# Weight units reordered and loaded at other places, and the context of the next tile moved to the tile's beginning, in a fused attention and ternary FFN kernel

## Chip, cores and metric

One Trainium2 chip, all 8 NeuronCores, one launch. Each core computes half of the rows of one batch element, with no traffic between cores. The metric is the device time of the slowest core in microseconds. The kernel before takes 1146.7 us, the median of 3 timed runs (1144.61 to 1150.81).

## The reference, cut to what matters

```python
x = hidden_states                     # (4, 4096, 1024), D = 1024, 16 heads of 64
h = layernorm(x)
q = softmax((h @ Wq.T + bq) @ Wfq.T + bfq)      # over all 1024 features
k = softmax((h @ Wk.T + bk) @ Wfk.T + bfk)
v = h @ Wv.T + bv
ctx = (q k^T / rowsum) v              # no softmax over positions: linear attention
x = x + ctx
a = act_quant(layernorm(x))           # 127 / max|row|, rounded
W' = weight_quant(W)                  # scale by 1/mean|W|, round, clip to -1, 0, 1
g = silu(a @ w_gate'.T); u = a @ w_up'.T        # INNER = 4096
x = x + act_quant(g * u) @ w_down'.T
```

Each weight matrix of the FFN can be quantised only when the mean of |W| over the whole matrix is known, so it has to be read through once for the mean and a second time for the quantised values.

## The kernel before

**Work and tiles.** A core holds 2048 rows of its own (16 tiles of 128, `TQ`) and also reads the other 2048 rows of its batch element, since keys and values need all 32 tiles (`TKV`). The first phase walks over 32 slots i. Slot i projects the values V(i) (from slot 8 on, `NE`), one of the items CQ(0) to CQ(8) that fold the two query matrices into one (slots 5 to 13, `cq_slot`), or the query logits Q(t) (slots 16 to 26), then the key logits K(i+1), and adds k^T v of tile i into PSUM (`pe_kv`, named KV below). An item is 16 matmuls of 128x512. VectorE adds the bias and takes the maximum, ScalarE takes the exponential (`ac_ek`, EK) and scales the values (`ac_ve`, VE). The second phase runs the FFN over the 16 own tiles: per tile 8 pairs G, U of 8 matmuls each (oc 0 to 7), and, from tile 3 on (`LAG` = 3), the down projection of the tile three back, 64 matmuls.

**Weight units.** The FFN weights come in 48 units of 1 MB each (16 per matrix; w = 0 gate, 1 up, 2 down). A unit (1, w, u) is pass 1: load it and let ScalarE sum |W| (`unit_ac`, an Abs of 1.9 us). A unit (2, w, u) is pass 2: load it again, let GpSimd scale it (`unit_gp`), and let ScalarE write the sign as fp8. Units 13 to 15 of gate and up are kept (`NRET` = 3, tile `keep`) between the passes, in the space that `wg8` and `wu8` take later, which is also the space of the attention weights and of `stage`. A kept unit's load therefore waits (`ready`, L378) for CQ(8) in the case of gate, and for the last two casts of the attention weights in the case of up. All other units rotate through 4 buffers `wst` (3 in the FFN phase), and the load of one waits until the one before it in its buffer has been used.

**Order.** `units` (L330 to L336) is one list. A planner (L346 to L352) puts its first 74 units into slots of the first phase by estimated slot length; the first 6 (`NPRE`) are handled ahead of the slots. With that rule the slots before hold 2 units in slots 5 to 7, 3 in slots 8 to 12, 3 in slot 13 (number 28, then the kept gate units 29 and 30), and about 3 in each of 16 to 26 and 2 in 27 to 29. The 22 remaining units go into FFN tiles 0 to 3 at the steps listed in `ffn_units` (L452). The matrix means are finished in a chain ScalarE, VectorE, TensorE, VectorE (`mean_dv1`, `mean_pe`, `mean_dv2`); `mean_at` (L459) puts it one slot after the matrix's last unit: slot 9 for up, slot 15 for gate. The mean of down stands in tile 1, at oc 1 on VectorE and after oc 2 on TensorE.

**Queues.** Every engine has one instruction list that it runs in order. SyncE issues nearly all loads (L751 to L763): in slot i first the activation tile i + 4, then the units of the slot. An issue whose semaphore isn't there yet holds all that stand behind it in SyncE's list. In the FFN ScalarE issues the loads of the down units itself, behind the unit three before.

**Steps touched in the FFN.** `pe_ctx(t+1)` computes the attention output of the next tile in 3 parts into PSUM banks `KB[0..2]`; `dv_ctx` normalises them and adds them to the residual (`cm`, `x2`). Before, they stand after oc 0 of tile t, and from tile 4 on (`t > LAG`) two parts share a bank, `KB[0]`, so part 2 waits for part 0's `cm`. `ac_hq` converts the previous tile's hidden values behind GpSimd's scaling (`gp_hr`) and, in tiles 1 to 3, stands ahead of the first two `ac_silu`.

## Time and profile before

| | value |
|---|---|
| timed runs, slowest core | 1146.7 us median (1144.61 to 1150.81, n = 3) |
| the profiled execution | 1136.11 us, span of its slowest core 1134.4 us |
| spans of the 8 cores in it | 1122.7 to 1134.4 us |
| TensorE matmul busy | 1071.1 us, 94% of the span |
| VectorE, ScalarE, GpSimd busy | 627.7, 500.3, 204.0 us |
| moved by DMA | 193.36 MB, mean 170 GB/s |

The profile is one execution on its slowest core, core 3. The 90 unit loads of 1 MB, the 20 MB of attention weights and most of the activations pass in the first 570 us. The profiled execution lies 10.6 us below the median of the timed ones.

### The profile page before, as it was taken

What the parts mean: (1) busy time and instruction counts of PE and PEld (TensorE: products, weight loads), DVE (VectorE), ACT (ScalarE), POOL (GpSimd) and SP (SyncE); (2) the same over time, 40 slices, a digit from 0 to 9 for tenths busy, and PEclk for the clock granted to TensorE, in tenths of its full rate; (3) what the DMA queues carried; (4) which work ended last, traced back from release to release, by engine and by line L of the source; (5) the groups of instructions that cost most, each with busy time, mean ns of one, the idle gap of its engine ahead of it and who ended that gap; (6) DMA issues with size and microseconds to landing.
All of it is one profiled execution on the core that took longest, in us unless ns stands there. A gap on an engine that the chain in (4) does not pass through costs nothing.

```text
span 1134.4 us, 13495 instructions; the slowest of 8 cores (1122.7 to 1134.4 us)
## 1 busy us (share of the span) xinstructions
PE 1071.1 (94%) x5414; PEld 501.3 (44%) x5414; DVE 627.7 (55%) x1133; ACT 500.3 (44%) x603; POOL 204.0 (18%) x132
## 2 busy tenths in 40 slices
PE   4898889979999999897989999999999999999998
PEld 2343444434444544343434444444444444444443
DVE  4525655566767667775745744644744644744311
ACT  3545867568888837465442222222222222222110
POOL 0000001022443320454322021021021021011010
PEclk9998999999999999899999999999999999999999
DMA  8996999669979966779961451451341341241240
GB/s 274 313 318 197 344 307 336 239 237 306 343 240 331 317 173 195 190 198 240 173 128 38 84 121 38 85 121 38 84 121 38 84 121 38 75 93 40 55 110 38
DMA packets 202318, 193.36 MB, mean 170 GB/s; under 512 B 169872, under 2 KB 173968, under 8 KB 194832
## 3 DMA queue, kind: packets, MB, share of 16 engines
q1 hardware_dynamic: 180448, 168.39, 53.3%
q10 hardware_dynamic: 21808, 24.12, 7.0%
q8 instruction: 42, 0.69, 0.3%
q14 instruction: 20, 0.16, 0.1%
HBM read 142.16 MB, written 29.36 MB: 151 GB/s over the span
## 4 chain that ended last, share of the span: by engine, by line
PE 65%; DVE 11%; ACT 10%; DMA 10%; issue 3%; POOL 1%; SPq 1%; ACTq 0%; DVEq 0%; POOLq 0%
PE ps L664 33%; PE ps L644 19%; PE ps L481 9%; DMA wst<-wuT 4%; ACT ek L1227 2%; DMA wst<-wdT 2%; ACT wst L411 2%; DVE nm L864 1%; DVE bnst L829 1%; ACT wu L425 1%; DVE lg L860 1%; DMA keep<-wuT 1%; ACT wg L425 1%; DVE hmid L1172 1%; ACT eq L1253 1%
## 5 line engine op out<-in xcount | busy, mean ns | idle before, releaser
L664 PE MATMUL ps<-wg,aqT 128*128 128x512 fp8e4 x1024 | 244.5, 382 | 4.1 <-DVE aqT L1139 2.6
L664 PE MATMUL ps<-wu,aqT 128*128 128x512 fp8e4 x1024 | 244.0, 381 | 2.3 <-DVE hmid L1172 2.2
L1296 ACT ACTIVATE silu<-ps,l 128x512 f32<-128x512 f32 x128 | 87.7, 686 | 325.8 <-PE ps L664 315.1
L1172 DVE SCALAR_TENSOR_TENSOR hmid<-ps,l,silu 128x512 f32<-128x512 f32 x128 | 95.8, 748 | 141.7 <-PE ps L664 109.0
L664 PEld LDWEIGHTS ps<-wu,aqT 128*128 128x128 bf16 x1024 | 100.5, 98 | 126.3 <-DVE hmid L1172 4.3
L664 PEld LDWEIGHTS ps<-wg,aqT 128*128 128x128 bf16 x1024 | 98.5, 98 | 117.3 <-DVE aqT L1139 3.8
L1346 POOL TENSOR_SCALAR hmid<-hmid,hsc 128x1024 f32<-128x1024 f32 x64 | 70.4, 1118 | 316.9 <-DVE hsc L1193 316.9
L481 PE MATMUL ps<-wck,xT 128*128 128x512 bf16 x512 | 121.5, 393 | 0.8 <-ACT vst L1244 0.8
L397 POOL TENSOR_SCALAR wst<-wst,msum 128x2048 f32<-128x2048 f32 x42 | 84.3, 2012 | 210.4 <-DMA wst<-wuT 112.6
L1164 DVE SCALAR_TENSOR_TENSOR xr<-ps,hsc,xr 128x512 f32<-128x512 f32 x32 | 24.0, 751 | 168.1 <-PE ps L644 168.1
L481 PE MATMUL ps<-wv,xT 128*128 128x512 bf16 x448 | 101.1, 379 | 0.0
L1306 ACT ACTIVATE hqs<-hmid 128x1024 bf16<-128x1024 f32 x64 | 66.9, 1056 | 70.3 <-POOL hmid L1346 69.0
L644 PE MATMUL ps<-wd,hqTa 128*128 128x512 fp8e4 x384 | 85.9, 384 | 3.7 <-ACT wd L425 3.7
L411 ACT ACTIVATE wst<-wst 128x2048 f32<-128x2048 f32 x42 | 79.9, 1903 | 12.9 <-DMA wst<-wuT 8.2
L481 PEld LDWEIGHTS ps<-wck,xT 128*128 128x128 bf16 x512 | 51.1, 102 | 66.2 <-issue 7.7
L1180 DVE TENSOR_REDUCE hmx<-hmid 128x1 f32<-128x1024 f32 x64 | 78.1, 1220 | 2.2
L1339 POOL TENSOR_TENSOR xr<-xr,bvb 128x1024 f32<-128x1024 f32 x16 | 37.6, 2354 | 183.4 <-DMA xr<-x_own 183.4
L644 PE MATMUL ps<-wd,hqTb 128*128 128x512 fp8e4 x320 | 69.9, 379 | 0.0
L481 PE MATMUL ps<-wfT,wnat 128*128 128x512 bf16 x256 | 60.1, 395 | 5.3 <-ACT wfT L311 2.2
L481 PEld LDWEIGHTS ps<-wv,xT 128*128 128x128 bf16 x448 | 42.7, 98 | 46.5
L644 PEld LDWEIGHTS ps<-wd,hqTa 128*128 128x128 bf16 x384 | 37.8, 99 | 50.8 <-ACT wd L425 4.7
L860 DVE TENSOR_TENSOR lg<-ps,bkc 128x1024 f32<-128x1024 f32 x32 | 39.0, 1218 | 36.8 <-PE ps L481 32.1
(107 smaller groups left out, 1112.9 us busy)
## 6 DMA issues: line engine op xcount, KB each, us to landing
wst<-wuT SPq DMA_DIRECT2D x26, 1024.0 KB, 12.5
wst<-wgT SPq DMA_DIRECT2D x26, 1024.0 KB, 11.2
wst<-wdT ACTq DMA_DIRECT2D x19, 1024.0 KB, 5.8
xr<-x_own SPq DMA_DIRECT2D x32, 512.0 KB, 6.9
s_hq<-hqs SPq DMA_DIRECT2D x32, 512.0 KB, 4.1
wst<-wdT SPq DMA_DIRECT2D x13, 1024.0 KB, 7.8
xr<-x_oth SPq DMA_DIRECT2D x16, 512.0 KB, 13.7
y<-xr SPq DMA_DIRECT2D x16, 512.0 KB, 3.4
```

The source lines that it names most:

```text
L397: gp(lambda e: e.tensor_scalar(b, b, msum[:, 4 + w:5 + w], ROUND32, op0=ALU.mult, op1=ALU.add), [at("unit", unit_id[1, w, u]) if wslot_of[ ...
L411: ac(lambda e: e.activation(o, b, ACTF.Abs, bias=0.0, scale=1.0, accum_out=absc[:, k:k + 1], saturate=False), [at("wld", n), last_junk[0] ...
L481: pe(lambda e, h=h, c=c, l_=l_, r_=r_: e.matmul(AB[b][:, 512 * h:512 * h + 512], l_, r_, start=(c == 0), stop=(c == CH - 1)), (list(after) ...
L644: pe(lambda e, c=c, b=b, o=o: e.matmul(KB[1 + h], b[:, o:o + 128], wd8[:, c * D + 512 * h:c * D + 512 * h + 512], start=(c == 0), stop=(c ...
L664: pe(lambda e, c=c: e.matmul(out, a[:, c * 128:c * 128 + 128], w8[:, c * DI + 512 * oc:c * DI + 512 * oc + 512], start=(c == 0), stop=(c = ...
L860: dv(lambda e: e.tensor_tensor(o, b, bias[...], op=ALU.add), after, done)
L1172: dv(lambda e: e.scalar_tensor_tensor(hmid[:, 512 * oc:512 * oc + 512], U[oc % 2], l2[:, s + 6:s + 7], sl, op0=ALU.mult, op1=ALU.mult), [a ...
L1180: dv(lambda e: e.tensor_reduce(hmx[:, s2 + k:s2 + k + 1], hmid[:, D * k:D * k + D], axis=AX, op=ALU.max, apply_absolute_value=True), [at(" ...
L1296: ac(lambda e: e.activation(silu[:, (oc % 2) * 512:(oc % 2) * 512 + 512], G[oc % 2], ACTF.Silu, bias=0.0, scale=l2[:, s + 5:s + 6]), [at(" ...
L1306: ac(lambda e: e.activation(hqs[:, g * D:(g + 1) * D], hmid[:, g * D:(g + 1) * D], ACTF.Copy, bias=-ROUND32, scale=1.0), [at("hr", t, g)] ...
L1339: gp(lambda e: e.tensor_tensor(xf(t), xf(t), bvb[...], op=ALU.add), [at("x2in", t), at("biases")], ("xb", t))
L1346: gp(lambda e: e.tensor_scalar(o, o, hsc[:, k:k + 1], ROUND32, op0=ALU.mult, op1=ALU.add), [at("hs", t)], ("hr", t, g))
```

## The change

Six edits, all in the order of work; no instruction of the arithmetic is added or dropped.

1. `NPRE` falls from 6 to 3: three units, not six, are read ahead of EK(0) on ScalarE, and three more move into the slots. Four casts of attention weights move ahead of the first key steps on VectorE.
2. The list `units` is reordered: the second-pass use of the kept up units now stands ahead of the first-pass reading of the kept gate units.
3. The loads of the kept units are issued in slot 3 (up) and slot 13 (gate), behind the slot's activation tile and ahead of the slot's other units.
4. The means of up and gate are taken two slots after the last unit, not one. By the planner's rule the slots become: slot 4: number 3; slots 5 to 7: two each; slot 8: 10, 11, 12; slot 9: the kept up units 13 to 15; slots 10 to 12: 16 to 24; slot 13: 25, 26, 27, 28; slot 14: 29, 30 (kept up, pass 2); slot 15: 31 and 32; slot 16: 33 to 35; slot 21: four units (48 to 51) where there were three; slot 29: three (71 to 73) where there were two. Mean of up in slot 11, of gate in slot 18.
5. In FFN tiles 1 to 3 the context of the next tile stands at the beginning of the tile, on TensorE and VectorE, in three separate banks, now for tile 4 also.
6. The mean of down is asked for at the start of tile 1 on VectorE and after oc 1 on TensorE. Tile 1 takes 5 down units where it took 4, tile 3 takes 5 where it took 6. In tiles 1 to 3 ScalarE puts the silu between the two `ac_hq` of the step.

```diff
@@ -33,7 +33,7 @@
 NWF = 3
 NP1 = 10
 NRET = 3
-NPRE = 6
+NPRE = 3
 LAG = 3
 NXF = 6
 
@@ -327,9 +327,11 @@
 
 
 
-    units = [(1, w, u) for w in (1, 0) for u in range(16)]
     kept = list(range(16 - NRET, 16))
-    own = [(2, w, u) for w in (1, 0) for u in kept + list(range(16 - NRET))]
+    rest = list(range(16 - NRET))
+    units = [(1, 1, u) for u in rest + kept] + [(1, 0, u) for u in rest]
+    units += [(2, 1, u) for u in kept] + [(1, 0, u) for u in kept]
+    own = [(2, 1, u) for u in rest] + [(2, 0, u) for u in kept + rest]
     for u in range(NP1):
         own[4 * u + 3:4 * u + 3] = [(1, 2, u)]
     units += own
@@ -451,12 +453,12 @@
 
     ffn_units = {}
     n1 = NA
-    for t, at_oc in enumerate([(1, 2, 3, 4, 5, 6), (3, 4, 6, 7),
-                               (2, 3, 4, 5, 6, 7), (2, 3, 4, 5, 6, 7)]):
+    for t, at_oc in enumerate([(1, 2, 3, 4, 5, 6), (2, 3, 4, 6, 7),
+                               (2, 3, 4, 5, 6, 7), (2, 3, 4, 5, 6)]):
         ffn_units[t] = {oc: n1 + k for k, oc in enumerate(at_oc)}
         n1 += len(at_oc)
     assert n1 == len(units)
-    mean_at = {unit_slot[unit_id[1, w, 15]] + 1: w for w in range(2)}
+    mean_at = {unit_slot[unit_id[1, w, 15]] + 2: w for w in range(2)}
 
     def xsrc(i):
         t, src = (i, x_oth) if i < TQ else (i - TQ, x_own)
@@ -646,7 +648,7 @@
                 wd8[:, c * D + 512 * h:c * D + 512 * h + 512],
                 start=(c == 0), stop=(c == 31)),
                [at("hqT", t, c // 16), at("unit", unit_id[2, 2, c // 2]),
-                at("y", t - 1, h) if t else at("cm", LAG, 1 + h)],
+                at("y", t - 1, h) if t else at("cm", LAG + 1, 1 + h)],
                ("down", t, h) if c == 31 else None)
 
     for p in range(3):
@@ -670,27 +672,30 @@
     WL = max(unit_id[2, w, u] for w in range(2) for u in range(16))
 
     def ctx_bank(t, part):
-        return KB[part] if t <= LAG else (KB[0], T, KB[0])[part]
+        return KB[part] if t <= LAG + 1 else (KB[0], T, KB[0])[part]
 
     for t in range(TQ):
+        if 0 < t <= LAG:
+            for k in range(3):
+                pe_ctx(t + 1, k, KB[k], at("cm", t, 2) if k == 0 else None)
         for oc in range(8):
             b = oc % 2
             pe_half(t, oc, G[b], wg8,
                     gfree[b] + [at("aqT", t), at("unit", WL)], ("G", t, oc))
             pe_half(t, oc, U[b], wu8, ufree[b], ("U", t, oc))
             gfree[b], ufree[b] = [at("silu", t, oc)], [at("h", t, oc)]
-            if t == 1 and oc == 2:
+            if t == 1 and oc == 1:
                 mean_pe(2, t_free[0])
                 t_free[0] = at("mean", 2)
-            if t + 1 < TQ and oc == 0:
-                pe_ctx(t + 1, 0, ctx_bank(t + 1, 0), at("cm", t, 2))
-                if t + 1 <= LAG:
+            if oc == 0 and (t == 0 or LAG < t < TQ - 1):
+                pe_ctx(t + 1, 0, KB[0], at("cm", t, 2))
+                if t == 0:
                     pe_ctx(t + 1, 1, KB[1], None)
                     pe_ctx(t + 1, 2, KB[2], None)
                 else:
                     pe_ctx(t + 1, 1, T, t_free[0])
                     t_free[0] = at("cm", t + 1, 1)
-            if LAG < t + 1 < TQ and oc == 1:
+            if LAG < t < TQ - 1 and oc == 1:
                 pe_ctx(t + 1, 2, KB[0], at("cm", t + 1, 0))
             if t + 1 < TQ and oc == 6:
                 pe_at(t + 1)
@@ -734,8 +739,7 @@
         unit_load(n)
     for n in range(NV, NV + 8):
         load_chunk(n)
-    for n in range(4, NPRE):
-        unit_load(n)
+    unit_load(4)
 
     def load_xf(t):
         if t < 4:
@@ -759,8 +763,13 @@
             load_x(i + 4)
         elif i >= TKV - 4:
             load_xf(i + 4 - TKV)
+        for w in (1, 0):
+            if i == (13, 3)[w]:
+                for u in kept:
+                    unit_load(unit_id[1, w, u])
         for n in slot_units[i]:
-            unit_load(n)
+            if n > 4 and wslot_of[n] is not None:
+                unit_load(n)
 
     def load_eld(t):
         free = (at("ctx", t - 2, 2) if t >= 2 else
@@ -995,23 +1004,26 @@
     cke(4)
     cke(5)
     unit_ac(1)
-    unit_ac(2)
     cke(6)
     cke(7)
-    for n in range(3, NPRE):
-        unit_ac(n)
+    unit_ac(2)
     dv(lambda e: e.tensor_tensor(bkc[...], bkc[...], AB[item_bank["BK"]],
                                  op=ALU.add),
        [at("BK"), at("bfk")], ("BKe",))
+    cast_chunk(NV)
+    cast_chunk(NV + 1)
     dv_tk(0)
+    cast_chunk(NV + 2)
     dv_tk(1)
+    cast_chunk(NV + 4)
     for i in range(TKV):
         dv_rz(i)
         if NE <= i + 2 < TKV:
             dv_xh(i + 2)
         if i < 4:
             for n in range(NV + 4 * i, NV + 4 * i + 4):
-                cast_chunk(n, "v")
+                if n not in (NV, NV + 1, NV + 2, NV + 4):
+                    cast_chunk(n, "v")
         if NE <= i + 3 < TKV:
             dv_stats(i + 3)
         if i in mean_at:
@@ -1194,16 +1206,20 @@
            [at("hc", t)], ("hs", t))
 
     for t in range(TQ):
+        if t == 1:
+            mean_dv1(2)
+        if 0 < t <= LAG:
+            for k in range(3):
+                dv_ctx(t + 1, k, ctx_bank(t + 1, k))
         for oc in range(8):
             dv_h(t, oc)
             if t == 1 and oc == 1:
-                mean_dv1(2)
                 mean_dv2(2)
             if t + 1 < TQ:
-                if oc == 0:
+                if oc == 0 and not 0 < t <= LAG:
                     dv_ctx(t + 1, 0, ctx_bank(t + 1, 0))
                     dv_ctx(t + 1, 1, ctx_bank(t + 1, 1))
-                if oc == 1:
+                if oc == 1 and not 0 < t <= LAG:
                     dv_ctx(t + 1, 2, ctx_bank(t + 1, 2))
                 if oc == 2:
                     dv_ln2a(t + 1)
@@ -1267,7 +1283,8 @@
         ac_ve(i)
         if i < 4:
             for n in range(NV + 4 * i, NV + 4 * i + 4):
-                cast_chunk(n, "a")
+                if n not in (NV, NV + 1, NV + 2, NV + 4):
+                    cast_chunk(n, "a")
         for n in us[0:1]:
             unit_ac(n)
         if NE <= i + 3 < TKV:
@@ -1316,12 +1333,8 @@
         for oc in range(8):
             if early and oc < 2:
                 ac_hq(t - 1, 2 * oc)
-                if oc == 0:
-                    ac_hq(t - 1, 1)
-                    ac_silu(t, 0)
-                else:
-                    ac_silu(t, 1)
-                    ac_hq(t - 1, 3)
+                ac_silu(t, oc)
+                ac_hq(t - 1, 2 * oc + 1)
             else:
                 ac_silu(t, oc)
             if t + 1 < TQ and oc == 5:
```

## Rows read from the trace of the kernel before

**Rows 1.** Cores: span and mean granted clock of some cores.

```profile
core 0: 1123.3 us, clock 0.991
core 3: 1134.4 us, clock 0.983
```

**Rows 2.** Who waited for whom, TensorE: line, releaser, us in total, times, longest us.

```profile
PE ps L435 <- DVE msum L430: 9.7, 3, 3.7
```

**Rows 3.** Short windows: busy us per engine (x instructions), granted clock, DMA share, GB/s.

```profile
96.00:100.00 4.00, 0.27 (x2) 0.00 (x0) 3.30 (x5) 1.46 (x3) 0.00 (x0) 0.80 0.00 0
212.00:216.00 4.00, 4.00 (x21) 1.81 (x19) 2.17 (x5) 3.49 (x6) 0.00 (x0) 1.00 0.02 4
220.00:224.00 4.00, 4.00 (x21) 1.78 (x19) 2.21 (x3) 1.32 (x1) 0.00 (x0) 1.00 0.96 360
```

**Rows 4.** Timeline of TensorE, slots 0 to 10: start, us, what, [idle before <- releaser].

```profile
101.64 1.05 PE L548 MATMUL ps<-vst,ek 128*128 128x129 bf16 x8 [5.37 <-ACT vst L1244]
...
167.02 0.59 PE L435 MATMUL ps<-msum,ones 128*128 128x1 f32 x2 [3.66 <-DVE msum L430]
...
174.78 3.62 PE L481 MATMUL ps<-wv,xT 128*128 128x512 bf16 x16
```

**Rows 5.** Timeline of ScalarE: a late unit before EK(0), the last kept up unit.

```profile
93.50 1.91 ACT L411 ACTIVATE wst<-wst 128x2048 f32<-128x2048 f32 x1 [1.12 <-DMA wst<-wuT]
...
161.45 1.91 ACT L411 ACTIVATE junk<-keep 128x2048 fp8e4<-128x2048 f32 x1 [1.37 <-DMA keep<-wuT]
```

**Rows 6.** SyncE's queue: what it waited for, and its issues around slot 13.

```profile
SPq L251 <- PE ps L481: 18.0, 1, 18.0
...
197.38 0.33 SPq L251 DMA_DIRECT2D wst<-wgT  x1
215.71 1.97 SPq L251 DMA_DIRECT2D keep<-wgT  x2
```

**Rows 7.** Timeline of ScalarE, slot 13: number 28, the second kept unit, EK(14).

```profile
213.43 1.90 ACT L411 ACTIVATE wst<-wst 128x2048 f32<-128x2048 f32 x1
...
225.24 1.91 ACT L411 ACTIVATE junk<-keep 128x2048 fp8e4<-128x2048 f32 x1 [0.56 <-DMA keep<-wgT]
...
227.15 1.13 ACT L1227 ACTIVATE ek<-lg,nm 128x1024 bf16<-128x1024 f32 x1
```

**Rows 8.** Timeline of TensorE: KV(14), the mean of gate, V(16).

```profile
229.90 0.64 PE L548 MATMUL ps<-vst,ek 128*128 128x129 bf16 x8 [2.95 <-ACT vst L1244]
...
237.58 0.38 PE L435 MATMUL ps<-msum,ones 128*128 128x1 f32 x2 [3.14 <-DVE msum L430]
237.82 5.30 PE L481 MATMUL ps<-wck,xT 128*128 128x512 bf16 x16
...
243.88 3.62 PE L481 MATMUL ps<-wv,xT 128*128 128x512 bf16 x16
```

**Rows 9.** Timeline of ScalarE in a query slot: two signs behind EQ.

```profile
336.01 3.89 ACT L425 ACTIVATE wg<-wst,cst 128x2048 fp8e4<-128x2048 f32 x2 [0.46 <-ACT eq L1253]
```

**Rows 10.** The chain that ended last: start, us, what, around the loads that TensorE waited for.

```profile
216.08 9.08 DMA keep<-wgT
...
378.80 11.72 DMA wst<-wgT
...
551.05 17.55 DMA wst<-wdT
```

**Rows 11.** Timeline of TensorE, FFN tiles 1 to 3 and the first down projection.

```profile
470.88 0.59 PE L435 MATMUL ps<-msum,ones 128*128 128x1 f32 x2 [2.91 <-DVE msum L430]
...
537.74 0.29 PE L623 MATMUL ps<-kvs,eld 128*128 128x130 bf16 x2 [4.44 <-DVE tmp L1061]
...
572.74 9.20 PE L644 MATMUL ps<-wd,hqTa 128*128 128x512 fp8e4 x34 [2.07 <-ACT wd L425]
```

**Rows 12.** Timeline of VectorE, tile 1: two equal residual adds of the context.

```profile
465.87 1.68 DVE L1067 TENSOR_TENSOR xr<-xr,tmp 128x384 f32<-128x384 f32 x1
...
468.28 0.56 DVE L1067 TENSOR_TENSOR xr<-xr,tmp 128x384 f32<-128x384 f32 x1
```

## Prediction

> **What bounds the kernel now.** I read in this order: cores, the engine table, TensorE's waits, then the timelines of TensorE, ScalarE and SyncE slot by slot, and last short windows for the DMA share. The slowest core needs 1134.4 us, the fastest about 11 us less, with clocks within 0.01 [rows 1]: the cores differ by their waits. TensorE is busy 94% of the span, so a gain can only come out of its stalls and out of the slow stretch that follows a stall. Those lie in two places. In slots 0 to 15 they end on late weight units or on a mean (9.7 us in three mean waits, the third of them in the FFN) [rows 2, 4, 8]. In FFN tiles 1 to 3 and the first down projection they end on the mean of down, on context part 2 (4.44 us) and on down weights [rows 11]. From tile 4 on TensorE doesn't stall and no edit reaches it. After a stall an item that takes 3.6 us otherwise took 5.30 [rows 8]: the granted clock there stood at the lower of its two levels, 1.2 GHz, as it does in a window after the first stall (0.80 on average, falling to half) [rows 3]. So a stall of 3 us costs about 5.
>
> The reader should see a third thing, since the change moves it: SyncE's queue. It waited once for 18.0 us for TensorE [rows 6]. That is the load of the kept gate units, held until CQ(8) ends at 215.5 us. In the windows before its end the DMA share is 0.02 [rows 3], and yet nothing stalled until then, because the loads up to number 28 had been issued at 197.4, ahead of the wait [rows 6], and ScalarE could begin number 28 at 213.4 [rows 7].
>
> **The change, part by part.** The sum stands against the profiled execution, 1136.1 us; the same difference is then put on the median of 1146.7, which lies 10.6 higher, as I find no term that would differ there.
>
> *Front, slots 0 to 10.* Before, EK(0) waits behind number 5, which ends at 95.4 [rows 5], and KV(0) begins at 101.64 after 5.37 us of idle [rows 4]. With three units ahead, EK(0) needs only the first maximum, some 3 us earlier, and so does KV(0). Four casts move forward, so three 0.5 MB chunks are fetched while the DMA queues stood empty (share 0.00 from 96 to 100) [rows 3]. But this is not yet time won, because slots 4 to 9 run at the pace of the loads. The volume up to the last up unit is the same as before. At 360 GB/s [rows 3] a unit takes 2.9 us and with the small transfers between them about 3.2. I counted the queue's idle time in the new order. It still idles until about 102, since chunk 35 needs a cast in slot 0. It idles again for nearly 4 us at about 110 to 114, because the kept up loads wait in slot 3 for the last cast with all later activation tiles and units behind them. That is 12 us of idle against 10.5. The last up unit (now number 12) lands at about 161 to 163, where before the last kept unit was begun at 161.45 [rows 5]. What is really won is the mean: TensorE idled 3.66 us for it at 167.0 [rows 4], and in slot 11 it will be there. But K(10) reuses the bank of V(9) and cannot start before about 166 for that reason, so only 1 us is left. I take −1.0 for the start of V(10) (174.78 before) [rows 4]. Bounds: +3, if the two idle stretches of the queue add up fully, and −6, the 3.66 with its slow item.
>
> *Slot 13.* This is the largest term, and it goes against the change. SyncE's list now reads: tile 17, three kept gate loads (wait for CQ(8)), then 25, 26, 27 and 28. Before, 25 to 28 stood ahead of that wait. ScalarE's list reads VE(13), 25, 26, 27, 28, EK(14), and behind EK(14) stand VE(14) and KV(14), at which TensorE stops. So all 7 MB must land after CQ(8) ends, call it T. First data flows about 2 us after the issue (kept load issued at 215.7, share 0.96 by 220) [rows 3, 6], then 7 x 2.9 = 20.3, then 2.1 for the last Abs: EK(14) starts at T + 24.4. KV(14) follows 2.75 later (227.15 to 229.90) [rows 7, 8], at T + 27.2. Before it was 229.90 - 215.5 = T + 14.4. The term is +12.8. Two kept loads took 9.08 us from issue to landing with small transfers between [rows 10], which agrees with 2.9 each. TensorE has items for 11 us after T and then stalls for some 16. Bounds: +9 (a rate of 420 GB/s and an early start) and +16 (3.4 us per unit).
>
> Here a rule of the Trainium skill speaks against the change. The row shows the queue silent for 18.0 us in front of one held load [rows 3, 6]. "DMA: Bandwidth & Descriptors", section "Anatomy of one DMA", says that a semaphore wait happens on the issuing sequencer before dispatch and that the DMA engines do not wait; the trace agrees. Were the wait held in the DMA queues instead, 25 to 28 would pass it and the whole change would gain about 13 us.
>
> *Slots 14 to 16.* The mean of gate moves from slot 15 to 18. Before, from KV(14) to V(16) it took 243.88 - 229.90 = 14.0 us, with 3.14 of idle and a slow item of 5.30 [rows 8]. Now V(15), slow after the stall (about 5.5), K(16) 3.5 and two short groups give 10.8. The term is −3.2, bounds −4 and −1.
>
> *Slots 21 and 29.* In the query slots the loop over ScalarE sets the pace: EQ, then the units, then EK. Two signs take 3.89 us behind EQ [rows 9]. A fourth unit in slot 21 adds one sign, +1.9 (bound 0 if EQ still waits). In slot 29 a third unit comes in ahead of EK(30); its load is issued after a unit of slot 28 and needs some 11.7 us [rows 10], so it just arrives, and its Abs adds +2.0 (bounds 0 and +3).
>
> *FFN tiles 1 to 3.* Ideal is 3.46 us per pair. Tile 1 (454 to 492) loses 2.91 of idle for the mean of down and 2.9 of slow matmuls behind it [rows 11]. The mean's first step now runs before VectorE's context work. What is late next: the first hidden product, which waits for the context. Its three parts take 6.1 us, since a residual add takes up to 1.68 while GpSimd runs, where an equal one takes 0.56 [rows 12]; TensorE then waits about 1.6 us for the buffer U. Net −5.0. Tile 2 starts from a VectorE that is less behind: it takes 33.1 us where 28.6 is ideal, and of these 4.5 us in small waits I take off 3. In tile 3 the 4.44 us for context part 2 [rows 11] and the slow pairs after it (1.8) go, since three banks are used; against it VectorE's context again stands ahead of the first product, 2.6. What is then late are the down units. The last one before was issued at 551.05 and took 17.55 us to land [rows 10], among the transposes of the hidden values; TensorE waited 2.07 for the last of them [rows 11]. With all tiles earlier, and one unit more fetched in tile 1, the last one lands some 12 us earlier by my count (about 557), and the first down projection ends near 569 instead of 581.8. The term is −12.5. Bounds: −17 (only 10 of the 27 us lost here remain) and −4 (the down loads do not come earlier; only tile 1's wait, less its new one, is kept).
>
> Sum: −1.0 + 12.8 − 3.2 + 1.9 + 2.0 − 12.5 = 0.0. So 1136.1 stays, and on the median 1146.7; I say 1147.
>
> **Rivals.** *A, slower: down weights take the place of the waits removed.* The 22 down units and the transposes share the queues, and loads issued among transposes took 17.55 us against 9.08 without [rows 10]. If TensorE reaches tile 3 earlier but the last down unit lands at most 4 us earlier than now, TensorE waits for it in the first down projection. It decides from the moment at which the last sign comes later than the 31st matmul of that projection. Then the FFN gives −5 and the sum is +7.5: 1154. For it: waits there on ScalarE's signs already [rows 11]. Against it: the DMA share in tiles 0 and 1 leaves room to fetch earlier.
>
> *B, faster: the front gives more.* If the earlier chunks and the kept up units, loaded before the rest, keep the queues full, then VE(9) comes 4 to 5 us earlier, and the stall in slot 13 is shorter by a faster burst (9 instead of 12.8). The sum is −8: 1139. For it: 10 us of empty queue before 102 [rows 3]. Against it: the wait for the last cast in SyncE's list.
>
> *C, the stall of slot 13 doesn't come.* It would need CQ(8) to end long before ScalarE reaches number 25. Before, CQ(8) ended 2.1 us after ScalarE began slot 13's first unit [rows 6, 7]. The sum would be −13: 1134. I give it little.
>
> **How the numbers follow.** Forecast (terms near their values, within 5 us of zero): 0.46. A with its neighbours (also a longer burst in slot 13): 0.27. B: 0.22. C: 0.05. The likeliest case has its own range of 1141 to 1152. For 8 in 10 the range must take in A's 1154 and B's 1139 with the bounds of slot 13 and of the FFN: 1137 to 1158. Differences under 0.5% (5.7 us) can't be told from none here. Faster by more: 0.27. Within: 0.46. Slower by more: 0.27.
>
> **What the changed kernel's profile would show.** Slot 13: ScalarE idle ahead of four Abs with the releaser DMA wst<-wgT, and TensorE idle for about 16 us before a KV with a slow item behind it. Mean waits of up and gate: gone. V(10) within 3 us of 174. KV(14) near 242, V(16) near 252 to 254. Tile 1: no wait for msum, a wait of 1 to 2 us for hmid. Tile 3: no wait for tmp. The first down projection ends about 0 to 2 us from 581.8 in absolute time. The prediction would be wrong first if the burst of slot 13 cost under 9 or over 16 us, next if the first down projection still waited over 5 us for a sign.

## The result, and the profile after

The changed kernel is slower. Its median is 1165.88 us (1161.16 to 1229.43, 4 runs), against 1145.65 us (1143.39 to 1150.81, 4 runs) for the kernel before on the same chip; the ratio is 1.0156, 95% interval 1.0104 to 1.0209. The prediction was 1147 us with a range of 1137 to 1158, so the time lies outside it. Some executions were disturbed, with a lower granted clock on part of the cores: the ratios here leave out those far above the rest, and of the profiled execution of b2_casts_only (below), whose cores 0, 1, 4 and 5 ran at about 0.81 up to 280 us, only the other four cores are read. The profiled execution took 1161.16 us. The head of its page, then two of its cores with span and mean granted clock:

```profile
span 1159.6 us, 13495 instructions; the slowest of 8 cores (1132.8 to 1159.6 us)
```

```profile
core 3: 1144.2 us, clock 0.982
core 4: 1159.6 us, clock 0.971
```

The slowest core is now core 4. The cores lie up to 27 us apart, where before it was 12. To see where the time comes from I read the same instants off TensorE's timeline of every core and took means over the eight cores of a profiled execution. KV(i) is the start of the 8 short matmuls of that name; "tile 4" is the start of FFN tile 4's matmuls, behind the first down projection. Means in us, and the difference on core 3 alone, the core from whose trace the prediction was made:

| stretch | before | after | difference | on core 3 | predicted |
|---|---|---|---|---|---|
| span start to KV(9) | 170.6 | 173.2 | +2.6 | −0.9 | −1.0 (at V(10)) |
| KV(9) to KV(13) | 45.1 | 45.2 | +0.1 | +0.1 | 0 |
| KV(13) to KV(14) | 10.7 | 26.2 | +15.5 | +16.7 | +12.8 |
| KV(14) to KV(18) | 46.3 | 44.8 | −1.5 | −1.1 | −3.2 |
| KV(18) to KV(22) | 46.6 | 49.1 | +2.5 | +3.8 | +1.9 |
| KV(22) to start of the FFN | 105.0 | 105.3 | +0.3 | +0.7 | +2.0 |
| FFN to tile 4 | 151.2 | 147.2 | −4.0 | −9.6 | −12.5 |
| all up to tile 4 | 575.6 | 591.2 | +15.6 | +9.7 | 0.0 |

Such means differ between two profiles of the same code. Up to the FFN b4_before_short_down (below) is the kernel before, instruction for instruction, and its KV(9) stands at 173.1, its start of the FFN at 428.5, where the kernel before has 170.6 and 424.3. A difference of 2 or 3 us between two single profiles is therefore not certain.

Behind tile 4 nothing differs: core 3 before needs 552.6 us from there (1134.4 − 581.8), core 4 after the same (1159.6 − 607.0). Three places carry the result.

*Slot 13.* Core 3 of the changed kernel: SyncE's issues, ScalarE, TensorE (start, us, what, [idle before <- releaser]), then windows as in [rows 3].

```profile
214.93 2.49 SPq L251 DMA_DIRECT2D keep<-wgT  x3
217.46 2.53 SPq L251 DMA_DIRECT2D wst<-wgT  x4
...
233.00 1.91 ACT L413 ACTIVATE wst<-wst 128x2048 f32<-128x2048 f32 x1 [20.22 <-DMA wst<-wgT]
...
241.15 1.91 ACT L413 ACTIVATE wst<-wst 128x2048 f32<-128x2048 f32 x1 [0.45 <-DMA wst<-wgT]
...
245.81 1.05 PE L550 MATMUL ps<-vst,ek 128*128 128x129 bf16 x8 [19.64 <-ACT vst L1260]
...
247.50 5.58 PE L483 MATMUL ps<-wv,xT 128*128 128x512 bf16 x16
```

```profile
212.00:216.00 4.00, 4.00 (x20) 1.79 (x19) 2.18 (x4) 0.78 (x2) 0.00 (x0) 1.00 0.02 4
216.00:220.00 4.00, 4.00 (x32) 2.32 (x31) 1.80 (x3) 0.00 (x0) 0.00 (x0) 1.00 0.73 221
220.00:224.00 4.00, 4.00 (x20) 1.83 (x19) 1.46 (x2) 0.00 (x0) 0.00 (x0) 1.00 0.99 311
224.00:228.00 4.00, 2.17 (x11) 0.78 (x8) 0.00 (x0) 0.00 (x0) 0.00 (x0) 1.00 0.96 260
228.00:232.00 4.00, 0.00 (x0) 0.00 (x0) 0.00 (x0) 0.00 (x0) 0.00 (x0) 0.87 1.03 307
232.00:236.00 4.00, 0.00 (x0) 0.00 (x0) 0.00 (x0) 2.64 (x5) 0.00 (x0) 0.50 0.99 332
236.00:240.00 4.00, 0.00 (x0) 0.00 (x0) 0.00 (x0) 3.05 (x3) 0.00 (x0) 0.50 0.95 380
```

The queue is empty until CQ(8) ends (share 0.02), and then seven loads are issued within 5 us. ScalarE, which before was at its first unit of the slot at 213 [rows 7], waits 20.22 us, and TensorE stands for 19.64. While it stood the granted clock fell to 0.50, the lower of its two levels (1.2 GHz), and the first item after the stall took 5.58 us instead of 3.6, as one did after a smaller stall before [rows 8].

*Slot 5.* Of this stall the prediction says nothing. Core 3, SyncE, VectorE, TensorE:

```profile
113.14 1.27 SPq L251 DMA_DIRECT2D keep<-wuT  x3
114.46 2.29 SPq L251 DMA_DIRECT2D xr<-x_oth  x2
...
129.04 1.29 DVE L838 BATCH_NORM_STATS2 bnst<-xr 128x6 f32<-128x512 f32 x2 [9.15 <-DMA xr<-x_oth]
...
131.72 5.44 PE L483 MATMUL ps<-wfT,wnat 128*128 128x512 bf16 x16 [11.05 <-DVE wcq L910]
```

Three kept up units are issued ahead of activation tiles. VectorE waits for a tile, and TensorE for a result that VectorE forms behind that wait. On the mean KV(4) comes 4.4 us earlier than before, and KV(5) 6.0 us later.

*FFN.* Who waited for whom, TensorE, from the start of the FFN to tile 4 (us in total, times, longest). First the kernel before, core 3:

```profile
PE ps L623 <- DVE tmp L1061: 4.4, 1, 4.4
PE ps L644 <- ACT wd L425: 3.7, 2, 2.1
PE ps L435 <- DVE msum L430: 2.9, 1, 2.9
```

Then the changed kernel, core 4:

```profile
PE ps L666 <- ACT silu L1313: 18.7, 3, 10.9
PE ps L646 <- ACT wd L427: 3.1, 1, 3.1
```

Core 3 of the changed kernel has the same kind of wait:

```profile
PE ps L666 <- ACT silu L1313: 11.8, 4, 6.0
```

The waits that the edits aimed at are gone: no `tmp` (context part 2), no `msum` (mean of down). Another takes their place, which the kernel before has on a small scale (1.4 us in total on core 3, 3.3 on core 4). It reads best as a chain, core 4 in tile 3:

```profile
555.62 1.97 POOL L399 TENSOR_SCALAR wst<-wst,msum 128x2048 f32<-128x2048 f32 x1 [17.11 <-DMA wst<-wdT]
...
557.63 2.00 ACT L427 ACTIVATE wd<-wst,cst 128x2048 fp8e4<-128x2048 f32 x1 [14.66 <-POOL wst L399]
...
560.13 0.69 ACT L1313 ACTIVATE silu<-ps,l 128x512 f32<-128x512 f32 x1 [0.51 <-ACT wd L427]
...
560.88 3.59 PE L666 MATMUL ps<-wg,aqT 128*128 128x512 fp8e4 x8 [10.89 <-ACT silu L1313]
```

A down unit's load lands late, GpSimd waits for it, the sign on ScalarE waits for GpSimd, and the silu that TensorE needs stands behind the sign in ScalarE's list.

The last of the 22 down units shows how the stream of loads as a whole moved. GpSimd's scaling of it on core 3, in the kernel before and in the changed one:

```profile
568.68 1.97 POOL L397 TENSOR_SCALAR wst<-wst,msum 128x2048 f32<-128x2048 f32 x1 [0.71 <-DMA wst<-wdT]
```

```profile
575.84 1.97 POOL L399 TENSOR_SCALAR wst<-wst,msum 128x2048 f32<-128x2048 f32 x1 [3.78 <-DMA wst<-wdT]
```

Counted from the core's own start of the FFN (426.9 and 446.2) these are 141.8 and 129.6 us, 12.2 less. On the mean of the cores they are 138.1 and 133.4, only 4.7 less, and tile 4 follows 13 to 14 us later (151.2 and 147.2), as the 64 matmuls of the first down projection alone take 13.98 us. So the end of this stretch moves with the stream of down loads, be it through a wait in the projection or through the silus ahead of it.

### The profile page after: what moved, and what is told of

It reads as the page before. It is cut to its first block, busy times and chain, and to the rows that moved or that the text cites. A ratio compares the mean times of both kernels' runs of the same rounds, so it can differ in the third digit from the quotient of the medians.

```text
span 1159.6 us, 13495 instructions; the slowest of 8 cores (1132.8 to 1159.6 us)
## 1 busy us (share of the span) xinstructions
PE 1069.4 (92%) x5414; PEld 502.3 (43%) x5414; DVE 616.4 (53%) x1133; ACT 499.4 (43%) x603; POOL 206.4 (18%) x132
## 4 chain that ended last, share of the span: by engine, by line
PE 64%; DMA 13%; ACT 10%; DVE 9%; issue 2%; POOL 1%; SPq 1%; ACTq 0%; DVEq 0%; POOLq 0%
PE ps L666 30%; PE ps L646 19%; PE ps L483 11%; DMA wst<-wdT 5%; DMA wst<-wuT 3%; DMA wst<-wgT 3%; ACT ek L1243 2%; DVE nm L873 1%; ACT wst L413 1%; DVE lg L869 1%; ACT wu L427 1%; ACT wg L427 1%; PE ps L513 1%; DVE bnst L838 1%; SPq L251 1%
## 5 line engine op out<-in xcount | busy, mean ns | idle before, releaser
L666 PE MATMUL ps<-wg,aqT 128*128 128x512 fp8e4 x1024 | 245.3, 383 | 20.8 <-ACT silu L1313 18.7
L483 PE MATMUL ps<-wck,xT 128*128 128x512 bf16 x512 | 118.7, 387 | 4.4 <-ACT vst L1260 4.4
L399 POOL TENSOR_SCALAR wst<-wst,msum 128x2048 f32<-128x2048 f32 x42 | 84.1, 2007 | 211.5 <-DMA wst<-wuT 105.0
L483 PE MATMUL ps<-wv,xT 128*128 128x512 bf16 x448 | 104.0, 387 | 0.0
L483 PE MATMUL ps<-wfT,wnat 128*128 128x512 bf16 x256 | 59.0, 390 | 14.6 <-DVE wcq L910 10.9
L483 PE MATMUL ps<-wcq,xT 128*128 128x512 bf16 x256 | 57.7, 379 | 1.1 <-DVE hmid L869 1.1
## 6 DMA issues: line engine op xcount, KB each, us to landing
wst<-wgT SPq DMA_DIRECT2D x26, 1024.0 KB, 10.9
```

What stands on the lines that cost most here:

```text
L399: gp(lambda e: e.tensor_scalar(b, b, msum[:, 4 + w:5 + w], ROUND32, op0=ALU.mult, op1=ALU.add), [at("unit", unit_id[1, w, u]) if wslot_of[ ...
L483: pe(lambda e, h=h, c=c, l_=l_, r_=r_: e.matmul(AB[b][:, 512 * h:512 * h + 512], l_, r_, start=(c == 0), stop=(c == CH - 1)), (list(after) ...
L666: pe(lambda e, c=c: e.matmul(out, a[:, c * 128:c * 128 + 128], w8[:, c * DI + 512 * oc:c * DI + 512 * oc + 512], start=(c == 0), stop=(c = ...
```

## The experiments

Each ratio is against the kernel before on the same chip. "Slot step" is KV(13) to KV(14), "FFN step" is start of the FFN to tile 4; all instants are means over the cores of a profiled execution.

### Which of the kept loads costs what

Edits on the changed kernel. e1 moves the kept gate loads behind the units of slot 13, e2 the kept up loads from slot 3 to behind the units of slot 8, e3 does both, a6 puts the gate ones between units 26 and 27. The edit of e3:

```diff
         for w in (1, 0):
-            if i == (13, 3)[w]:
+            if i == {}.get(w):
                 for u in kept:
                     unit_load(unit_id[1, w, u])
         for n in slot_units[i]:
             if n > 4 and wslot_of[n] is not None:
                 unit_load(n)
+        for w in (1, 0):
+            if i == {0: 13, 1: 8}.get(w):
+                for u in kept:
+                    unit_load(unit_id[1, w, u])
```

> The changed kernel with one edit: in slot 13 the three kept gate loads are issued behind units 25 to 28, not ahead of them. Queue theory: the 19.6 us stall at KV(14) on core 3 was the wait of 25 to 28 behind the held loads; they now go out about 17 us before CQ(8) ends, ScalarE finds them there, and KV(14) comes at 229 to 232 us (245.8 in the changed kernel), 14 to 17 us earlier; the whole kernel 1149 to 1153. Rival (slot too full): the four Abs of slot 13 and their 4 MB are too much for the slot wherever the loads stand; KV(14) stays above 238 and the kernel within 5 us of 1165.

> The changed kernel with one other edit: the three kept up loads are issued behind the units of slot 8, not in slot 3. Queue theory: activation tile 8 is no longer behind 3 MB and a held load, the 11 us stall of TensorE in slot 5 goes (CQ(1) at about 125 instead of 131.7), but the same bytes must be there before slot 10, so KV(9) is the same within 2 us of 172.9 and the kernel within 3 us of 1165. Rival: the stall in slot 5 is real loss, KV(9) comes 5 us or more earlier and the kernel gains as much.

> Both edits together. Queue theory: FFN start at 430 to 433 us on core 3 (446.2 in the changed kernel, 426.9 before), what is left against before being the fuller slots 18, 21 and 29; the kernel 1148 to 1153. Rival (slot too full): within 5 us of 1165.

> The changed kernel with the three kept gate loads of slot 13 not ahead of all four units 25 to 28, but between 26 and 27. From KV(13) to KV(14) the changed kernel takes 24 to 33 us by core, with the kept loads behind all four 7.8. Theory S (each MB that stands in SyncE's list behind the held load costs its own transfer and its share of ScalarE's passes, about 3.5 us): five MB instead of seven must land after the hold, so KV(14) comes 7 us earlier, the step is 18 to 21 us, ratio about 1.009. Rival H (the hold itself costs: any unit of the slot behind it brings the whole delay, since the rate at the start of the burst and not the count sets it): the step stays over 23 us, ratio 1.014 to 1.016.

| kernel | ratio, interval | KV(9) | slot step | FFN step | tile 4 |
|---|---|---|---|---|---|
| changed | 1.0156 (1.0104 to 1.0209) | 173.2 | 26.2 | 147.2 | 591.2 |
| e1_gate_behind | 0.9908 (0.9850 to 0.9966) | 172.1 | 7.8 | 148.6 | 571.6 |
| e2_up_behind | 1.0059 (1.0015 to 1.0104) | 160.6 | 26.9 | 148.9 | 582.6 |
| e3_both_behind | 0.9869 (0.9825 to 0.9913) | 160.6 | 8.4 | 148.2 | 562.3 |
| a6_two_ahead | 1.0088 (1.0042 to 1.0135) | 170.8 | 19.7 | 145.6 | 581.4 |

The gate loads cost 18.4 us of the slot step (26.2 − 7.8), the up loads 12.6 us of KV(9) (173.2 − 160.6). At tile 4 the two add up: e1 is there 19.6 us before the changed kernel, e2 8.6, e3 28.9. The expectations held for the places and missed the amounts. In e1 the queue theory had the slot right (KV(14) at 230.2 on core 3, expected 229 to 232), but the medians of e1 and e3, 1137.0 and 1126.58 us, came out far below the 1149 to 1153 and 1148 to 1153 expected. In e2 its expectation failed, that KV(9) would stay within 2 us, and the rival held: the stall of slot 5 was real loss.

In e3, core 3, nothing that is needed soon stands behind the held loads any more:

```profile
186.79 10.86 SPq L251 DMA_DIRECT2D wst<-wgT  x4
201.51 1.42 SPq L251 DMA_DIRECT2D keep<-wgT  x3
...
213.64 0.64 PE L550 MATMUL ps<-vst,ek 128*128 128x129 bf16 x8 [0.88 <-ACT vst L1264]
```

The hold for CQ(8) is also shorter there, 3.8 us on SyncE against 19.5 in the changed kernel. That its length is not what costs is shown by the kernel before: its hold took 18.0 us [rows 6], with a slot step of 10.7.

a6 gives the price of one load. With two units ahead of the hold, ScalarE's last unit of the slot starts 18.7 us after the issue of the kept loads (232.97 − 214.31, core 3), with none ahead 26.2 us (241.15 − 214.93): 3.8 us for each of the two megabytes. The mean over the cores is 6.5 / 2 = 3.25 us. Theory S holds (step 19.7, ratio 1.0088): the delay goes by what stands behind the hold.

### The front: three units ahead, the casts, the spread

a7 is the kernel before with `NPRE = 3` and the four early casts, b1 with `NPRE = 3` alone, b2 with the casts alone. c1 leaves six ahead of the first keys and spreads the rest over slots 6 to 29; from slot 6 on each slot then has the units that it has in b1, and 13 instead of 16 stand ahead of KV(9). The first edit is that of a7 and b1, the second that of c1:

```diff
-NPRE = 6
+NPRE = 3
...
-        want = sum(slot_len[:4]) + (n + 1 - NPRE) * sum(slot_len[4:]) / (
+        want = sum(slot_len[:6]) + (n + 1 - NPRE) * sum(slot_len[6:]) / (
```

> The kernel before with three units ahead of the first keys and the four early casts alone; order of the units, kept loads, place of the means and FFN are as before. KV(9) starts at 167.4 to 173.9 us in the kernel before (mean 170.7) and at 156.8 to 165.3 (mean 160.4) in e3_both_behind. Theory F (the gain of the front is the earlier chunk loads in the empty queue and the shorter list ahead of the first keys): KV(9) at 161 to 165 on the mean, ratio about 0.993. Rival M (it is the mean asked for a slot later and the kept up loads out of the way that gave it; what is fetched earlier only waits earlier): KV(9) stays over 168, ratio 0.997 to 1.0.

> The kernel before with three weight units ahead of the first keys instead of six and nothing else. Means over the cores: KV(9) starts at 170.6 in the kernel before and at 160.6 in a7_front_only, which has this and the four early casts. Theory N (the units ahead are the cost: their loads and passes stand in front of chunks, casts and the first keys): KV(0) 2.5 to 3 us earlier and KV(9) at 161 to 163, ratio about 0.987. Rival K (the early casts are what keeps the load queue filled): KV(0) earlier by as much, but KV(9) over 168, ratio 0.997 to 1.0.

> The kernel before with the four early casts and six units ahead as it has. Theory N (units ahead are the cost): KV(9) stays over 168 on the mean of the cores, ratio 0.997 to 1.003. Rival K (casts): KV(9) at 161 to 164, ratio about 0.987. Third case (each gives a part, 3 to 7 us): both were needed, the ratios are 0.991 to 0.996 for both kernels.

> The kernel before with six units ahead of the first keys, but the other 68 spread over slots 6 to 29 instead of 4 to 29. From slot 6 on every slot has the units that it has in b1_three_ahead, and 13 instead of 16 are asked for ahead of KV(9). Theory D (the number of megabytes that ScalarE's list demands ahead of KV(9) sets it, at the pace of the loads): KV(0) as in the kernel before, at 101 on the mean, and KV(9) at 161 to 164.5 where the kernel before has 170.6; ratio about 0.987. Rival K0 (what counts is that the first keys don't wait for number 5): KV(9) stays over 167.5, ratio 0.996 to 1.0.

| kernel | ratio, interval | KV(0) | KV(9) | between | slot step |
|---|---|---|---|---|---|
| before | 1 | 101.0 | 170.6 | 69.6 | 10.7 |
| a7_front_only | 0.9846 (0.9785 to 0.9908) | 98.1 | 160.6 | 62.5 | 8.2 |
| b1_three_ahead | 0.9777 (0.9593 to 0.9960) | 99.3 | 163.6 | 64.3 | 7.8 |
| b2_casts_only, cores 2, 3, 6, 7 | 1.0015 (0.9956 to 1.0073) | 101.3 | 168.7 | 67.4 | 10.4 |
| c1_late_spread | 0.9945 (0.9912 to 0.9979) | 103.6 | 167.8 | 64.2 | 8.2 |

a7, the first edit alone, gains more than its theory F expected (KV(9) at 160.6 against 161 to 165, ratio 0.9846 against 0.993). The casts alone change the time by nothing that can be told (b2, 1.0015). At KV(9) they come with 2.3 us (171.0 in the kernel before on the same four cores) and beside three units ahead with 3.0 (a7 against b1), which is within what two profiles of the same code differ by. Three units ahead give 7.0 us at KV(9), where the expectation was about 8 to 10. c1 bears on how. From KV(0) to KV(9) it is as fast as b1 (64.2 and 64.3 against 69.6), though six still stand ahead of the first keys; those 5.3 us go with asking for three megabytes less ahead of KV(9). But as its KV(0) came 2.6 us later than before, for a reason that I did not find, only 2.8 us are left at KV(9), and its expected 161 to 164.5 was missed; 167.8 lies in the rival's range, the ratio 0.9945 in neither. So the demand explains a part, and how large a part isn't shown. ScalarE's waits for loads from 100 to 176 us, core 3 of the kernel before:

```profile
ACT junk L411 <- DMA keep<-wuT: 7.1, 3, 5.5
ACT wst L411 <- DMA wst<-wgT: 2.7, 3, 1.6
```

The same of b1:

```profile
ACT wst L411 <- DMA wst<-wuT: 6.4, 3, 3.4
ACT junk L411 <- DMA keep<-wuT: 2.7, 2, 1.5
```

The wait for the kept up units before (7.1 us, longest 5.5) stands ahead of EK(9) in slot 8. In b1 they are asked for in slot 9, and only 2.7 us of waiting is left.

### The place of the mean

> Kernel e3_both_behind with the means of up and gate asked for one slot behind their last unit, as in the kernel before, instead of two. Theory W (the later question is what takes the waits of 3.66 and 3.14 us and the slow item after each away): two waits for msum of 3 to 5 us come back, ratio 0.9869 + 0.006 = about 0.993. Rival E (with the loads on time the sums are ready within one slot, and the second slot gives nothing): no wait for msum over 1.5 us in slots 9 to 18, ratio within 0.002 of 0.987.

```diff
-    mean_at = {unit_slot[unit_id[1, w, 15]] + 2: w for w in range(2)}
+    mean_at = {unit_slot[unit_id[1, w, 15]] + 1: w for w in range(2)}
```

Measured: 0.9792 (0.9705 to 0.9880), tile 4 at 562.5 (e3: 562.3). On core 2 the waits of TensorE from 150 to 270 us are

```profile
PE ps L550 <- ACT vst L1264: 1.5, 1, 1.5
PE ps L483 <- ACT vst L1264: 1.0, 1, 1.0
PE ps L437 <- DVE msum L432: 0.4, 1, 0.4
```

On every core the wait for the mean is 0.4 to 0.5 us in all (0.5 to 1.6 in e3), so rival E holds for the waits; its ratio, 0.987 within 0.002, is inside the measured interval, though 0.9792 itself is lower. The waits of 3.66 and 3.14 us before [rows 4, 8] were late units seen through the mean; once the units are on time, asking a slot later gains nothing.

### The FFN

e4 is the kernel before with the FFN edits alone. a5 is e3, and b4 the kernel before, each with short down loads; b3 is e3 with a plain transfer in place of the transposing one.

```diff
+        src = unit_src(w, u)
+        if n >= NA:
+            dst, src = dst[:, 0:1, 0:512], src[:, 0:1, 0:512]
...
-        spt(f"dG{h}", b[:, o:o + 2048], r,
+        sp(f"dG{h}", b[:, o:o + 2048].rearrange("p (c k) -> p c k", k=128),
+           r.rearrange("(c n) k -> n c k", n=128),
```

> The kernel before with only the edits of the FFN (context at the beginning, mean of down earlier, 5 and 5 down units in tiles 1 and 3, silu between the conversions). If the FFN edits are worth what core 3 showed (FFN start to tile 4: 154.9 before, 145.3 after), the kernel is 6 to 10 us faster than before, 1136 to 1140. Rival (down units bound): the time from FFN start to tile 4 on the slowest core stays at 152 to 158 us, as on core 4 of the changed kernel (158.2), since ScalarE's silu stands behind a sign that waits for its load; then the kernel is within 4 us of before.

> Kernel e3_both_behind, in which each of the 22 down units of the FFN loads only a quarter of its rows' half (0.25 MB or less instead of 1 MB); the rest of the buffer is stale, so the down weights and the output are not the reference's, and the arithmetic is the same in amount. From the start of the FFN to the start of tile 4, e3_both_behind takes 141 to 155 us by core, 148.2 on the mean of the eight. Theory L (silu stands on ScalarE behind a sign whose unit's load is late): without late loads the span is 138 to 142 on all cores, no wait of TensorE for silu over 2 us in tiles 1 to 3, ratio to the kernel before about 0.979. Rival V (VectorE's context and layer-norm work sets the pace of these tiles, the late signs only fill its slack): the span stays within 3 us of 148, ratio about 0.986.

> The kernel before, in which each down unit of the FFN loads only a quarter (output not the reference's), as in a5_short_down. The span from the start of the FFN to tile 4 is 151.2 on the mean in the kernel before and 132.1 in a5_short_down. Theory G (the waits that the FFN edits remove are those I counted, and late loads hide their gain): the span is 142 to 146 here, so that without late loads the edits are worth the 10 to 14 us that I predicted; ratio about 0.993. Rival W (the waits on the mean and on context part 2 are themselves a consequence of late signs): the span is 132 to 136 here too, so the edits are worth under 4 us either way; ratio about 0.984.

> Kernel e3_both_behind, in which the hidden values come back from memory by a plain transfer of the same bytes instead of a transposing one; they are in the wrong places, so the output is not the reference's. Down units whose loads are issued beside the transposes need about 23 us for three (issued 462.2, landed 485.0 on core 2). Theory T (the transposing transfers hold the DMA engines): these loads land within 12 us, the span from the start of the FFN to tile 4 falls from 148 toward the 132 of a5_short_down, to 132 to 138, ratio 0.972 to 0.978. Rival B (the 22 MB of the eight cores at once are what takes the time, whoever else uses the queues): the loads still need over 18 us, the span stays over 144, ratio 0.984 to 0.988.

| FFN step (ratio of the kernel) | whole down loads | short down loads | cost of late loads |
|---|---|---|---|
| FFN part before | 151.2 (1) | 147.3 (0.9846, 0.9707 to 0.9986) | 3.9 |
| FFN part changed | 148.2 in e3 (0.9869) | 132.1 (0.9659, 0.9586 to 0.9732) | 16.1 |
| worth of the edits | 3.0 | 15.2 | |

e4 itself took 147.2 us in this step, 4.0 under before, with a ratio of 0.9969 (0.9901 to 1.0036): the 6 to 10 us expected did not come, and the rival's "within 4 us of before" did. The direction is certain: five profiled kernels with the FFN part of before take 150.8 to 154.2 us in this step, eight with the changed one 145.6 to 149.1. In substance theory G holds, though b4's step of 147.3 us lies just outside its 142 to 146 and b4's ratio of 0.9846 is lower than its 0.993. The gain that I counted is there (15.2 us, predicted 12.5), but only where the loads aren't late; rival W, with 132 to 136 in b4, is excluded. a5 has the changed front too; a kernel before with only the FFN edits and short loads was not run. The waits of TensorE in the FFN step, core 3 of b4, which has the FFN part of before:

```profile
PE ps L667 <- DVE hmid L1175: 3.9, 3, 3.1
PE ps L438 <- DVE msum L433: 2.9, 1, 2.9
PE ps L626 <- DVE tmp L1064: 2.3, 1, 2.3
PE ps L637 <- ACT aq L1135: 2.2, 2, 1.1
```

The same of a5, which has the edits:

```profile
PE ps L669 <- DVE aqT L1158: 2.0, 1, 2.0
PE ps L639 <- ACT aq L1151: 1.1, 1, 1.1
PE ps L669 <- DVE hmid L1191: 0.8, 1, 0.8
```

In a5 the silu waits are gone, and the step of 132.1 is shorter than the 138 that I had expected at best. b3 (0.9714, 0.9487 to 0.9940) took 142.1 us in the step, which lies between its two theories. Transfers of the hidden values without transposing take 6 of the 16 us away; their size stayed, so what I can say is that the transposing is part of the cause. The other part goes with the loads' own volume. The last down unit reaches GpSimd 135.1 us after the start of the FFN in e3, 128.8 in b3 and 113.1 in a5 (means). GpSimd's waits for down units in e3, core 2 (us in total, times, longest):

```profile
POOL wst L399 <- DMA wst<-wdT: 48.0, 7, 20.6
```

and in b3, core 2:

```profile
POOL wst L399 <- DMA wst<-wdT: 38.8, 7, 10.9
```

The longest wait halves on this core; over the eight it is 8.6 to 21.3 us in e3 and 6.6 to 11.2 in b3. The transposes of the query exponentials (queue, count, median us to landing) in e3, core 2:

```profile
eld<-s_eq SPq DMA_TRANSPOSE x4, 16.6
```

and in a5, core 2:

```profile
eld<-s_eq SPq DMA_TRANSPOSE x4, 6.1
```

With short loads a transpose lands in 6.1 us instead of 16.6; the medians of the eight cores from 408 to 572 us are 4.4 to 6.2 us in a5 and 4.9 to 16.6 in e3. So each kind of transfer is longer beside the other.

### Two more tries on the best kernel

> Kernel a8_mean_one_slot with the down units at the positions of the kernel before (four in tile 1, six in tile 3) instead of the changed ones (five and five). The span from the start of the FFN to tile 4 is 148.9 on the mean in a8_mean_one_slot. Theory P (the early sign in tile 1 starts a load sooner and helps): 151 to 154, ratio over 0.982. Rival Q (loads are the limit, and their positions only choose which silu waits): within 2 us of 148.9, ratio 0.978 to 0.981.

c2 puts the down units where the kernel before has them: 0.9813 (0.9769 to 0.9858), FFN step 146.9 against 148.9 in a8. Rival Q holds for the step, within 2 us; that the positions only choose which silu waits was not read from the trace.

> Kernel a8_mean_one_slot with its 71 units spread over slots 5 to 29 instead of 4 to 29, so that 12 instead of 13 are asked for ahead of KV(9). Theory D: KV(9), at 161.4 on the mean in a8_mean_one_slot, comes 2 to 3.5 us earlier, at 158 to 159.5, and half of it or more is kept to the end, ratio about 0.977. Rival F (TensorE's own work is the limit of these slots by now): KV(9) within 1 us of 161.4, ratio 0.979 or more.

c3 spreads the units of a8 over slots 5 to 29 (`slot_len[:5]`, `slot_len[5:]`). It came out at 1.0032 (0.9991 to 1.0073). KV(9), at 160.1, was 1.3 us earlier, between what its two theories expected, but the next four slots took 55.0 us instead of 45.2, and KV(14) to KV(18) 51.7 instead of 42.5. Core 0, SyncE, then ScalarE:

```profile
141.94 1.67 SPq L251 DMA_DIRECT2D keep<-wuT  x3
143.66 0.43 SPq L251 DMA_DIRECT2D xr<-x_oth  x1
144.13 0.63 SPq L251 DMA_DIRECT2D wst<-wuT  x1
...
170.06 1.91 ACT L413 ACTIVATE wst<-wst 128x2048 f32<-128x2048 f32 x1 [9.94 <-DMA wst<-wuT]
```

The spread moved unit 12 into slot 9, while the kept loads stayed at slot 8 by their number. They now stand ahead of a unit that is needed first, whose load took 25.9 us to land here. That is the fault of the changed kernel once more, made by me. What the stretch behind KV(14) lost, I didn't take apart.

The best kernel of the study is a8: the changed kernel with its kept loads behind the units and the mean one slot after its last unit, ratio 0.9792 (0.9705 to 0.9880). e3, c2 and a7 can't be told from it by their ratios, and a7 is only the first of the six edits. One end stays open: the ratios often moved more than the profiled instants (a7 is 10.3 us earlier at tile 4, and its ratio of 0.9846 is some 17 us). A part of it may be that the profiled execution of the kernel before lay 10.6 us under its median.

## Why the prediction was wrong, step by step

The sum was 0.0, and the same terms measure +15.6 us on the mean of the cores; the median moved by 20.2. On core 3, from which every row of the sum was read, they measure +9.7. The misses are these.

*FFN tiles 1 to 3* (−12.5 predicted, −4.0 measured) is the largest, 8.5 us, and the step that failed is its last one. I summed the removed waits and then wrote that the last down unit would land "some 12 us earlier by my count". The list of removed waits was right, as a5 against b4 shows. The landing came out on core 3 (12.2 us, counted from the start of the FFN), but that core was one of the latest before. On the mean it was 4.7 us (138.1 to 133.4), and 3.0 in e3. That is one unit in 6.3 us before and one in 6.1 after, with TensorE's own waits removed, and the end of the stretch moved with the units (−4.0). I had also put at nothing what the earlier units do: silus stand behind their signs. They cost 11.8 us of waiting on core 3, which still won 9.6, and 18.7 on core 4, the slowest. Tile by tile on core 3, tile 1 took 6.4 us less (predicted 5.0), tile 2 3.5 more, where I had taken 3 off, and tile 3 with the projection 6.7 less. The bound of −4 named just this case, "only tile 1's wait, less its new one, is kept", and I should have given it more weight: the row of 17.55 us for one load [rows 10] spoke for it.

*Rival A* had the cause and its price (−5) and an eye on the wrong place. It asked for a last down unit "at most 4 us earlier" (measured 4.7 on the mean) and looked for the wait at the first down projection. That projection in fact ran through on core 3, and waited 3.1 us on core 4. The greater wait came earlier, at silus that stand behind a sign.

*Slot 13* (+12.8; +15.5 against the kernel before, 18.4 against e1) was right in its mechanism, and the term mis-sized in the rate. I took 2.9 us per megabyte from a window at 360 GB/s [rows 3]; the windows after show 221 to 332 GB/s up to 236 us and 380 in the next one, 302 on the mean or 3.5 us per megabyte, and a6 3.25 to 3.8. My own row could have said so: two kept loads in 9.08 us [rows 10], less the 2 us to first data, are up to 3.5 us each, not the 2.9 that I took them to confirm. My bound of +16 had 3.4 in it.

*Rival C* (no stall) is excluded by the 19.64 us row. The sentence from the Trainium skill beside this term, that waits are held on the issuing sequencer ("DMA: Bandwidth & Descriptors", section "Anatomy of one DMA"), agrees with the slot step of the changed kernel, a6 and e1: 26.2, 19.7 and 7.8 us, by what stands behind the held issue. That section describes DMAs issued by GpSimd; for those of SyncE it is these rows that show it.

*Front* (−1.0; +2.6 on the mean of this pair, −0.9 on core 3). V(10) began at 173.87 on core 3, as forecast, and over three profiles each with the same code up to there (before, b4, e4; after, e1, a6) KV(9) is at 172.0 in both. So the size was right within what can be told, but by luck: two effects of 11 us cancel, and I had neither. I argued by the volume up to the last up unit, and that it doesn't change. Two things decide instead: how many megabytes stand ahead of the engine's next step in its own list, and which small transfers stand behind large ones in the queue. By the first, three units ahead are worth 7 us (b1), by the second the kept up loads cost 12.6 (e2 against the changed kernel, and 11.5 between e1 and e3). I had seen that "all later activation tiles and units" stand behind the kept up loads, but costed only the wait for the cast. *Rival B* saw the direction of the first, but not that the kept up loads eat it.

*Slots 14 to 16* (−3.2) came out at −2.5 on core 3, and 1.4 of it was given back in slot 18, where the mean is now asked for:

```profile
287.93 0.38 PE L437 MATMUL ps<-msum,ones 128*128 128x1 f32 x2 [1.01 <-DVE msum L432]
```

*Slot 21* (+1.9) cost 4.0 us on core 3, as the later first item after the wait ran slow (5.31 us); the mean of that stretch is +2.5. *Slot 29* (+2.0) cost 2.0 on core 3, but on the mean the stretch from KV(22) to KV(30) is level (79.0 and 79.1). Both terms stand at `NPRE = 3`, which shifts the whole spread: a7, without any other part of the change, shows the same 49.4 us from KV(18) to KV(22).

*Slowest core.* The metric follows the slowest core, and in the profiled executions that one lost 25.2 us (1159.6 − 1134.4) where the mean of the cores lost 15.6 and core 3 9.7. Had all cores moved as core 3 did, the median would have come to about 1156, an estimate from these numbers. Late loads hit the cores unequally: tile 4 starts at 570 to 582 us before and at 580 to 607 after. I had put nothing there.

## What to carry to other kernels

A load that is held must be issued behind everything that is needed before it. Its position in the issuing list cost about 3.5 us here for each megabyte that was needed behind it, and it has to be checked again after each change of a planner's numbers. Ask for each engine's step how many megabytes its own list demands ahead of it; moving three later gained 7.0 us at KV(9) (b1), filling an empty queue no more than 2 to 3, not clear of noise. When waits are removed from a stretch that also streams data through a few buffers, read first when the last load of the stream is used, on every core: if the stretch ends just one fixed piece of work later, as here (138.1 and then the 13 us of the down projection), the stream is the pace, and the gain turns into a wait at whatever stands behind it. And a term read from one core's trace is a forecast for that core: read the same rows on the others before it is added to a sum for the slowest.

## What the runs showed of the hardware

With seven megabytes queued at once on every core, one core's rate was 221, 311, 260, 307, 332 and 380 GB/s in windows of 4 us, at a DMA share of 0.95 to 1.03 from the second on: a full share does not mean a full rate. 1 MB loads and transposing transfers of eight cores lengthened each other: on core 2 GpSimd waited up to 20.6 us for one down unit beside transposing transfers and up to 10.9 beside one kind of them less, and a transpose that landed in 6.1 us beside short loads took 16.6 beside whole ones.
